# One constant of the work planner, BURST, from 2 to 1: contexts of an attention kernel are taken one key tile at a time

## What is computed

```python
mod = (_silu(L0_c) @ L0_wmod).reshape(L0_c.shape[0], 6, 1, -1)
sa, ca, ga, sb, cb, gb = (mod[:, 0], mod[:, 1], mod[:, 2], mod[:, 3], mod[:, 4], mod[:, 5])
h = _layernorm(x, axis=-1) * (1 + ca) + sa
x = x + ga * _L0_attn_ref(h, L0_attn_W_query, L0_attn_W_key, L0_attn_W_value, L0_attn_W_proj, L0_attn_b_proj)
h = _layernorm(x, axis=-1) * (1 + cb) + sb
x = x + gb * _L0_ffn_ref(h, L0_ffn_W_r, L0_ffn_W_k, L0_ffn_W_v, L0_ffn_mu_r, L0_ffn_mu_k)
...
h = _layernorm(x, axis=-1) * (1 + ca) + sa
x = x + ga * _L1_attn_ref(h, L1_attn_Wq, L1_attn_Wk, L1_attn_Wv, L1_attn_Wo)
h = _layernorm(x, axis=-1) * (1 + cb) + sb
x = x + gb * _L1_ffn_ref(h, L1_ffn_W, L1_ffn_b, L1_ffn_lora_down, L1_ffn_lora_up, L1_ffn_down_aux, L1_ffn_up_aux)
```

## Time and profile before

| what | value |
|---|---|
| median of 3 runs | 2966.63 us (2961.32 to 2970.31) |
| the profiled execution | 2965.31 us, span of its core 2963.6 us |
| TensorE matmuls busy | 2516.6 us, 85% of the span |
| VectorE busy | 2316.5 us, 78% |
| ScalarE busy | 1711.3 us, 58% |
| GpSimd busy | 843.0 us, 28% |
| mean granted TensorE clock | 0.944 of full speed |

### The profile page before, as it was taken

The page is one execution under the profiler, slowest core; times in us unless marked ns, Lnnn a source line. Parts: engine busy times, 40 slices in busy tenths (PEclk is TensorE's granted clock), DMA queues, the critical chain, the costliest instruction groups (busy, mean ns, idle before and its releaser), DMA issues.

```text
span 2963.6 us, 55344 instructions
## 1 busy us (share of the span) xinstructions
PE 2516.6 (85%) x19096; PEld 1074.0 (36%) x19096; DVE 2316.5 (78%) x7126; ACT 1711.3 (58%) x3458; POOL 843.0 (28%) x954
## 2 busy tenths in 40 slices
PE   5679788889869999799979899799997999888686
PEld 3313333333423434343333434334343433433323
DVE  4388776889878698878988788887988789884792
ACT  1346556656546566566665665665665666565364
POOL 3111252233122241223321242222512233225111
PEclk8779999999989999899999999899998999999898
DMA  5511124111322124122222213231132222302300
GB/s 172 162 47 55 35 69 119 58 46 48 108 81 76 48 60 124 51 76 79 86 88 64 86 48 92 78 95 45 48 115 74 76 63 79 96 28 58 98 2 15
DMA packets 141771, 218.37 MB, mean 74 GB/s; under 512 B 20438, under 2 KB 61932, under 8 KB 141428
## 3 DMA queue, kind: packets, MB, share of 16 engines
q1 hardware_dynamic: 141496, 214.83, 24.2%
HBM read 137.93 MB, written 77.89 MB: 73 GB/s over the span
## 4 chain that ended last, share of the span: by engine, by line
PE 51%; DVE 29%; ACT 7%; issue 4%; SPq 3%; DMA 3%; POOL 2%; DVEq 0%; ACTq 0%; POOLq 0%
PE ctx_ps L1479 11%; DVE small L1249 10%; PE big L1404 10%; PE big L1460 9%; PE small L1438 8%; PE big L1393 6%; DVE mx L1247 5%; ACT probs L1033 4%; PE big L1516 4%; PE big L1493 2%; SPq L866 2%; DVE stats L1198 2%; DMA lo_dram<-region 2%; DVE mx L1249 2%; DVE region L1308 1%
## 5 line engine op out<-in xcount | busy, mean ns | idle before, releaser
L1033 ACT ACTIVATE probs<-big 128x512 f32<-128x512 f32 (+2 forms) x2560 | 1219.5, 564 | 513.6 <-PE big L1460 508.2
L1249 DVE CUSTOM_DVE_ANT_0 small<-small,mask 128x128 f32<-128x128 f32 (+3 forms) x2048 | 941.8, 520 | 205.9 <-PE small L1438 196.3
L1460 PE MATMUL big<-stack_q,stack_k 64*128 64x512 f16 (+3 forms) x6144 | 693.8, 328 | 99.8 <-ACT probs L1033 61.1
L1247 DVE TENSOR_REDUCE mx<-small 128x1 f32<-128x512 f32 x1024 | 649.9, 684 | 104.8 <-PE small L1438 97.2
L943 POOL TENSOR_SCALAR_AFFINE_SELECT probs<-probs 128x512 f32<-128x512 f32 x512 | 328.6, 649 | 1382.8 <-ACT probs L1033 1382.6
L1438 PE MATMUL small<-stack_k,stack_q 64*128 64x512 f16 (+3 forms) x3072 | 467.5, 342 | 207.3 <-DVE mx L1249 150.4
L1479 PE MATMUL ctx_ps<-probs,v_ones 128*17 128x512 f32 (+3 forms) x6144 | 623.8, 500 | 7.2 <-POOL probs L943 4.0
L1460 PEld LDWEIGHTS big<-stack_q,stack_k 64*128 64x128 f16 x6144 | 255.7, 94 | 442.0 <-issue 237.6
L1438 PEld LDWEIGHTS small<-stack_k,stack_q 64*128 64x128 f16 x3072 | 122.4, 94 | 762.2 <-DVE mx L1249 391.8
L1249 DVE DVE_READ_ACCUMULATOR2_ANT mx<- 128x1 f32 x2048 | 285.4, 139 | 0.0
L1393 PE MATMUL big<-hT,w_qkv 128*128 128x512 f32 x512 | 267.2, 637 | 10.2 <-DMA w_qkv<-wqkv 4.3
(11 more groups left out here) (93 smaller groups left out, 2003.7 us busy)
## 6 DMA issues: line engine op xcount, KB each, us to landing
image<-region SPq DMA_DIRECT2D x192, 256.0 KB
stack_q<-image SPq DMA_DIRECT2D x64, 512.0 KB, 3.7
stack_k<-image SPq DMA_DIRECT2D x64, 512.0 KB, 4.6
lo_dram<-region SPq DMA_DIRECT2D x64, 256.0 KB
w_qkv<-wqkv SPq DMA_DIRECT2D x16, 768.0 KB, 4.9
x_res<-x SPq DMA_DIRECT2D x32, 256.0 KB, 4.9
stack_q<-lo_dram SPq DMA_DIRECT2D x128, 64.0 KB, 3.9
stack_k<-lo_dram SPq DMA_DIRECT2D x128, 64.0 KB, 5.0
```

Source lines behind the costliest of these rows:

```text
L1033: s.activation(probs[:, n % HELD, heads, q0:], big[:, at.slot(turn), 0:len(pairs) * width] .rearrange("p (h q) -> p h q", h=len(pairs)), A ...
L1247: last = v.reduce_max(to, held, AX)
L1249: last = v.tensor_tensor_reduce(out=held, in0=held, in1=mask[:, BANK - width:], scale=1.0, scalar=3.0 * NEG, op0=ALU.add, op1=ALU.max, acc ...
L1460: last = te.matmul(big[:, at.slot(at.turn() + parity), j * width:(j + 1) * width], stack_k[rows, c, g * PAIR_N + pair, kt * P:(kt + 1) * P ...
```

## The change

```diff
-BURST = 2
+BURST = 1
```

## The result

| | before | after |
|---|---|---|
| median | 2966.19 us (2961.32 to 2970.31, 4 runs) | 3034.4 us (3033.28 to 3037.89, 4 runs) |
| ratio to before | 1 | 1.0233, 95% interval 1.0215 to 1.0251 |
| span of the profiled execution | 2963.6 us | 3036.2 us |
| contexts in a row (runs of contexts) | 570 | 605 |
| TensorE matmuls busy / rest of the span | 2516.6 / 447.0 us | 2557.0 / 479.2 us |

The change costs 68 us, 2.3%. I had forecast 2981 us with a range up to 3022: the sign was right, the size was a fifth of the truth, and the result lies outside the range.

The account below looks back on a forecast made before the run. TensorE was taken as the bound in most places, VectorE's maxima elsewhere. Terms +16 + 10 - 8 = +18 us, times 0.8, gave +14 us: median 2981 us, forecast's own range 2970 to 3010, overall range 2930 to 3022.

Parts of the forecast that it names:

- What bounds the kernel: Whole kernel: TensorE bounds most places, VectorE's row maxima the rest; periodic middle, so order changes count about seven times.
- Part 1, shape changes: TensorE: 70 of 100 contexts taken earlier lose a join, each new run costing 0.23 us: +16 us.
- Part 2, own waits: TensorE: contexts taken earlier wait for their own probabilities, 100 x 0.1 us: +10 us.
- Part 3, filled waits: TensorE: contexts with finished probabilities fill 41 waits, 24 us at most, a third taken: -8 us.
- Part 4, what else moves: Saves on ScalarE and norms on VectorE follow each block's last context; hidden under TensorE work, costed at nothing.
- the rival that gains: Filled waits at layer-norm beginnings also avoid the 1.2 GHz clock afterwards: four waits, 15 us; chance of whole rival 0.28.
- Starved VectorE: Contexts step ahead of maxima where VectorE bounds, 198 more runs: +62 us, 3029 us; chance 0.12.
- Nothing to speak of: Planner prices, not the pair rule, decide when contexts are taken; few items move: 2967 us, 2960 to 2974; chance 0.15.
- filled waits: Contexts fill TensorE waits at layer-norm beginnings and the clock stays up: 2928 us in full, likely 2946; chance 0.28.
- the order of other items: Sign of being wrong: TensorE's row count of contexts stays but time moves; priced by none of the parts.

Follow-up runs that it names:

- s1: Kernel before, with 38 joins of contexts dissolved by moving the second context behind the next maximum: 2974.67 us, ratio 1.0036.
- the table of the orders: Kernels before and changed, each also with the planner's shape-change charge at 60, 66, 76, 80 instead of 71.86: 2949.1 to 3051.0 us.
- r1: Changed kernel with rows items moved ahead of the layer-norm items they stood right behind (8 places): 3033.12 us, ratio 1.0233.
- both edits: Changed kernel with rows items moved ahead of layer-norm items and ScalarE's two hi copies moved behind a score: 3014.95 us, ratio 1.0173.
- n6: Changed kernel (BURST = 1, no pairs) with the planner's shape-change charge at 76 instead of 71.86: 2949.1 us, ratio 0.9952.
- n7: Kernel before (BURST = 2, pairs) with the planner's shape-change charge at 66 instead of 71.86: 3051.0 us, ratio 1.0288.
- n4: Changed kernel (BURST = 1, no pairs) with the planner's shape-change charge at 60 instead of 71.86: 3007.0 us, ratio 1.0133.
- n2: Changed kernel (BURST = 1, no pairs) with the planner's shape-change charge at 80 instead of 71.86: 2964.2 us, ratio 1.0005.
- n3: Kernel before (BURST = 2, pairs) with the planner's shape-change charge at 60 instead of 71.86: 2991.3 us, ratio 1.0080.

## Why the prediction was wrong, point by point

**What bounds the kernel.** Right as a reading: TensorE first, VectorE second. The shares of the chain moved by one or two points only, so the profile's shares would not have shown 68 us coming. The change is not paid in every period, as I had it: the first third of the kernel costs nothing.

**Part 1, shape changes.** Mechanism right, count off by a factor of two. 35 more runs came, not 70; the last two of the kernel still stand together as said. At the 0.28 us that s1 measured they cost 10 us, not 16. The number of contexts taken early was about right: in the list 61 runs begin with one tile scored, where 6 did, and 205 with two, where 157 did. They lose fewer joins than I let them.

**Part 2, own waits.** The number was right in part by luck. The groups of L1479 and L1438 after, with idle time behind the second bar, against 7.2 us in the earlier trace rows:

```profile
L1438 PE MATMUL small<-stack_k,stack_q 64*128 64x512 f16 (+3 forms) x3072 | 473.5, 346 | 198.9 <-DVE mx L1249 103.2
L1479 PE MATMUL ctx_ps<-probs,v_ones 128*17 128x512 f32 (+3 forms) x6144 | 631.2, 500 | 20.2 <-POOL probs L943 11.1 <-ACT ctx_u L1043 7.1 <-ACT probs L1033 1.6
```

13 us more, where I had 10. Of these 13, contexts that wait for their own probabilities are 7 us (4.0 + 1.4 before, 11.1 + 1.6 after). The other 6 are waits for ScalarE to copy the bank out (1.2 before, 7.1 after), which is no part of this term.

**Part 3, filled waits.** Wrong in sign. I took -8 us from the waits that I found in the trace of before, as if they would stay while contexts moved into them. The new order has other waits: the periods of after have 3.5, 3.7 and 4.4 us where I had the 3.3 us go, and idle time grew by 32 us. A list of waits belongs to the order that it was read from.

**Part 4, what else moves.** This is the step that failed. I wrote of the saves and norms that they "follow", and costed all that else moves at nothing; even the 41.1 us that ScalarE waits for contexts became 63.7. In fact 5990 of the 7233 places of the list hold another item, rows came to stand behind layer norms in eight places, and a score behind a ScalarE that waits for a DMA. The idle time before scores went from 99.8 to 143.8 us, and I had no term for it:

```profile
L1460 PE MATMUL big<-stack_q,stack_k 64*128 64x512 f16 (+3 forms) x6144 | 700.6, 333 | 143.8 <-DVE m_lo L1267 44.7
```

The two kinds of long wait in it are examples and not the whole of the 68 us, as the repairs showed. What the runs put in place of my nothing is the table of the orders: 30 us on the average, with a spread of 34, for a new order. The trace of before shows the waits of one order and could not give this. The kernel could have given some of it: the planner is part of it, and with BURST = 1 it yields the list with its 5990 changed places, its 605 runs and its own end, 2617 us against 2574, before anything is measured. None of that is in the forecast.

**The clock.** I used the clock only in the rival that gains, where shorter waits would give 15 us back. The same reasoning holds the other way round, and it was the largest single part of the two traces: 45 us, or 37 at the highest clock of after. I had the row for it and looked at it from one side.

**The rivals.** Starved VectorE, at 3029 us, is the nearest number, and its mark appeared: VectorE's waits for maxima went from 293.5 us to 355.6 us, from the waits of VectorE after:

```profile
DVE mx L1247 <- PE small L1438: 178.6, 114, 12.4
DVE small L1249 <- PE small L1438: 177.0, 117, 43.6
```

But its mechanism was contexts in front of maxima, 198 more runs of them; with 35 more, that price is 11 us. That VectorE starved because TensorE stood before scores is only in part borne out: with the wait for rows gone (r1) VectorE still waits 356.3 us for maxima, and with both edits 332.2. "Nothing to speak of" and "filled waits" did not happen in this order, though the time of the second (2946 us) came, by luck, in n6 (2949); whether by filled waits is not shown.

**The mark that came nearest.** The last sentence of the prediction named "the order of other items", for a row count that stays while the time moves. The count did not quite stay, but 35 runs are 10 to 12 us of 68. It had no price and some 0.06 of chance. The ten orders show that it should have been the main case, with a spread of about 35 us.

What stays open: whether pairing is worth anything on the average (five against five values do not tell), and how the remaining 49 us of the change divide among its waits. The one wait that was removed whole only showed the next, so I don't think that all of it can be put down to single places, but that is argued, not shown; the table of idle time and clock is what the runs support.

The planner's own clock was a better sign than I had thought. It ends the list of before at 2574 us and of the change at 2617, 43 us later, which is the right side and not far from 68; n6 has 2586 and n7, the slowest, 2623. But n4 at 2580 ran 3007 us, and n2 and n3, both at 2599, ran 2964 and 2991. Over the ten the correlation with the measured time is 0.60. So it says something of an order and does not rank neighbours.

## What to carry to other kernels

Where a greedy planner fixes the order of everything, an edit of one rule is mostly a new draw of the order: compare the rule over several draws (turn a constant that has nothing to do with it) before believing that the rule did it, and put the spread of the draws into the range of a forecast. If a planner has a clock of its own, read what it says of both lists first, as a hint. A wait that is named in the trace costs its time only if no other wait takes its place when it is gone; test it by repairing it, and look whether the repair removed it. A long wait of TensorE costs its length and, here, the low clock at it, so any price for idle time should have both.

## What the runs showed of the hardware that I had not expected

Useless work can be free: 30 us of products in five waits of TensorE cost nothing (the median fell by 10 us), and the same products ten items later cost 34 us. And going to another array shape and back cost 0.28 us a run (0.16 to 0.41) in a list where only 38 contexts were moved.
